# Linear attention on one core: the two signs of a head on the two halves of the partitions

## What is computed

```python
DIM, HEADS, DH, G = (192, 12, 64, 4)
def _phi(x): return concatenate([relu(x), relu(-x)], axis=-1)      # 64 -> 128 features
k = (x @ Wk) ; v = (x @ Wv)                                        # per head 64 columns
q = einsum('bhnd,gde->gbhne', x @ Wq[g], Wt) + bt
q = _ln(gelu(q), gt, betat)
qf, kf = _phi(q) / sqrt(2 * DH), _phi(k)
kv = einsum('bhnd,bhnm->bhdm', kf, v)                              # a table per head: 128 x 64
out = einsum('gbhnd,bhdm->gbhnm', qf, kv)
norm = einsum('gbhnd,bhd->gbhn', qf, kf.sum(axis=2))
out = out / (norm + 1e-6)
fused = gelu(_ln(out @ Wf + bf, gf, betaf)); result = fused @ Wo + bo
```

## Time and profile before

| | |
|---|---|
| median of 3 runs | 2717.93 us (2717.76 to 2718.2) |
| the profiled execution's own time | 2718.29 us |
| its span (first to last instruction) | 2716.4 us |
| busy: PE, DVE | 2542.6 us (94%), 2483.3 us (91%) |
| busy: ACT, POOL | 1392.7 us (51%), 1350.4 us (50%) |
| mean granted TensorE clock | 0.96 |
| L914, table products | 11520 matmuls |
| L1013, features | 640 instructions, mean 672 ns, 384.8 us busy |
| `kv_now` copies | 40 DMAs of 390 KB, 2.6 us to landing |

### The profile page before, as it was taken

One profiled execution on the slowest core, in us unless ns is written; L12 is line 12 of the kernel. 1 busy time (PEld: TensorE's weight loads), 2 busy tenths in 40 slices (PEclk: granted clock), 3 DMA queues, 4 the chain that ended last, 5 costly groups with the idle time before them and its releaser, 6 DMA issues. The chain is left out here.

```text
span 2716.4 us, 74938 instructions
## 1 busy us (share of the span) xinstructions
PE 2542.6 (94%) x29336; PEld 1722.5 (63%) x29336; DVE 2483.3 (91%) x3770; ACT 1392.7 (51%) x2302; POOL 1350.4 (50%) x1019
## 2 busy tenths in 40 slices
PE   4999999788879999999999999999999999999577
PEld 2777777555546666666666666666666666666335
DVE  6999999888889999999999999999999999999583
ACT  5676766555545545545444545545444544554231
POOL 0000000555556666666666666666666766666210
PEclk8999999899989999999999999999999999999765
DMA  7321210211100000000000000000000000000001
GB/s 153 96 51 36 51 35 18 62 36 41 35 7 14 10 8 12 6 12 6 12 6 12 6 12 12 6 12 6 12 6 12 6 12 12 6 12 7 6 0 58
DMA packets 45139, 62.39 MB, mean 23 GB/s; under 512 B 4416, under 2 KB 36160, under 8 KB 44760
## 3 DMA queue, kind: packets, MB, share of 16 engines
q1 hardware_dynamic: 43928, 61.07, 8.5%
q10 hardware_dynamic: 1152, 0.51, 0.1%
HBM read 41.66 MB, written 3.93 MB: 17 GB/s over the span
## 5 line engine op out<-in xcount | busy, mean ns | idle before, releaser
L1231 POOL TENSOR_TENSOR phi_lo<-phi,phi_hi 128x1024 bf16<-128x1024 f32 x240 | 511.2, 2130 | 459.8 <-DVE phi_hi L1112 459.8
L1022 ACT ACTIVATE o_hi<-ps_u 128x512 bf16<-128x512 f32 x240 | 143.3, 597 | 705.1 <-PE ps_u L927 705.1
L941 PE MATMUL ps_y<-staging,o_hi 128*128 128x384 bf16 x1920 | 470.4, 327 | 9.6 <-DVE o_lo L1134 1.9
L941 PE MATMUL ps_y<-staging,o_lo 128*128 128x384 bf16 x1920 | 469.0, 326 | 0.0
L941 PE MATMUL ps_y<-wf_lo,o_hi 128*128 128x384 bf16 x1920 | 468.9, 326 | 0.0
L1224 POOL TENSOR_TENSOR q_ssq<-q_ssq,half 128x8 f32<-128x8 f32 x240 | 405.9, 1691 | 18.8
L1013 ACT ACTIVATE phi<-ps_t,betat,gt 128x512 f32<-128x512 f32 (+1 forms) x640 | 384.8, 672 | 0.8 <-PE ps_t L896 0.8
L1090 DVE SCALAR_TENSOR_TENSOR shared<-q_sum,shared 128x512 f32<-128x512 f32 x240 | 374.3, 1559 | 1.4
L154 PE MATMUL acc<-w_b,feat 128*128 128x384 bf16 x1728 | 295.5, 331 | 42.8 <-DVE w_b L266 39.4
L154 PEld LDWEIGHTS acc<-w_b,feat 128*128 128x128 bf16 x1728 | 168.5, 99 | 158.3 <-DVE w_b L266 40.0
L941 PEld LDWEIGHTS ps_y<-staging,o_lo 128*128 128x128 bf16 x1920 | 187.8, 98 | 124.2
(11 more groups left out here) (218 smaller groups left out, 5664.4 us busy)
## 6 DMA issues: line engine op xcount, KB each, us to landing
kv_now<-kvs SPq DMA_DIRECT2D x40, 390.0 KB, 2.6
xt<-in_x_dram SPq DMA_DIRECT2D x32, 320.0 KB, 5.5
wf_f<-in_wf_dram SPq DMA_DIRECT2D x24, 384.0 KB, 3.2
xt<-in_x_dram SPq DMA_DIRECT2D x32, 256.0 KB, 6.0
out_dram<-h SPq DMA_DIRECT2D x8, 480.0 KB, 2.9
staging<-in_wq_t_dram SPq DMA_DIRECT2D x1, 3072.0 KB, 11.0
staging<-in_tok_w_dram SPq DMA_DIRECT2D x12, 192.0 KB, 8.8
staging<-in_kv_w_dram SPq DMA_DIRECT2D x1, 1536.0 KB, 15.3
```

Source lines behind the costliest of these rows:

```text
L941: last = nc.tensor.matmul(ps_y[:, n, 0:HC], lhs, w[part][:, c, n * HC:(n + 1) * HC], start=c == 0 and lhs is oh and part == 'wf_hi', stop= ...
L1022: nc.scalar.activation(o_hi[:, j % 2], ps_u[:, 0:OC], ACT.Copy).then_inc(s["o_hi_done"], 1)
L1231: nc.gpsimd.tensor_tensor(phi_lo[:, j % 2], phi[:, j % 2], phi_hi[:, j % 2], ALU.subtract).then_inc(s["phi_lo_done"], 1)
```

## The change

The two signs of a head are put on the two halves of the partitions, so that a head's features fill all 128 rows. `features` has to move them there: for each part of an octet (one or two groups), each of the two heads and each of the two signs it has an instruction that reads 64 partitions and writes 64 partitions. The table products then take 128 rows at once. The matmuls read the tables straight from `kv_hi` and `kv_lo` at the batch of the tile; `kv_now` and its DMAs are gone. `accumulate` is changed to match: one matmul makes both signs of a head, with 128 columns of the stationary side.

```diff
@@ accumulate (keys_and_values)
-                    for j in range(HH // 2):
-                        for sign in range(2):
-                            for n, (k, v) in enumerate(((kf_hi, v_hi), (kf_hi, v_lo), (kf_lo, v_hi))):
-                                for side in range(2):
-                                    c = 2 * j + sign
-                                    last = nc.tensor.matmul(
-                                        ps_kv[side * DH:(side + 1) * DH, hf, c * KVW:(c + 1) * KVW],
-                                        k[:, m, 2 * j + side, sign, :], v[:, m, 2 * j + side, :],
...
+                    for j in range(HH):
+                        for n, (k, v) in enumerate(((kf_hi, v_hi), (kf_hi, v_lo), (kf_lo, v_hi))):
+                            last = nc.tensor.matmul(ps_kv[:, hf, j * KVW:(j + 1) * KVW],
+                                                    k[:, m, j].rearrange("p s d -> p (s d)"), v[:, m, j, :],
...
@@ attend
-            @block.sync
-            def _(sp):
-                def tables(tile):
-                    if (n := earlier(tile, NO - 1, NO, NO)) is not None:
-                        sp.wait_ge(s["attended"], n)
-                    sp.dma_start(kv_now[:, :, :, :, :], kvs[:, batch_of(tile.t)]).then_inc(s["kv_in"], 16)
...
@@ attend_octet
-                    if j == 0:
-                        pe.wait_ge(s["kv_in"], 16 * count(tile, 0, 1))
-                    for i in range(PAIRS):
-                        pair = (PAIRS * j + i) % HP
-                        for sign in range(2):
-                            for n, (feature, table) in enumerate(((phi_hi, 0), (phi_hi, 1), (phi_lo, 0))):
-                                for a in range(2):
-                                    rows = slice(a * DH, (a + 1) * DH)
-                                    last = nc.tensor.matmul(
-                                        ps_o[:, a, i * KVW:(i + 1) * KVW],
-                                        feature[rows, j % 2, sign, i * P:(i + 1) * P], kv_now[rows, table, pair, sign, :],
...
+                    b = batch_of(tile.t)
+                    for i in range(OCT):
+                        hd = (OCT * j + i) % HEADS
+                        c = i % PAIRS
+                        out = ps_o[:, i // PAIRS, c * KVW:(c + 1) * KVW]
+                        ph, pl = (v[:, j % 2, i // 2, i % 2, :] for v in (phi_hi, phi_lo))
+                        nc.tensor.matmul(out, ph, kv_hi[:, b, hd, :], start=c == 0, stop=False, skip_group_check=True)
+                        nc.tensor.matmul(out, ph, kv_lo[:, b, hd, :], start=False, stop=False, skip_group_check=True)
+                        last = nc.tensor.matmul(out, pl, kv_hi[:, b, hd, :], start=False, stop=c == PAIRS - 1,
+                                                skip_group_check=True)
@@ features (ACT)
-                    for sign in range(2):
-                        for g, a, b in groups(j):
-                            last = nc.scalar.activation(
-                                phi[:, j % 2, sign, a * P:b * P], ps_t[:, a * P:b * P], ACT.Relu,
-                                bias=w['betat'][:, sign, g:g + 1], scale=w['gt'][:, sign, g:g + 1])
+                    for g, a, b in groups(j):
+                        for head in range(2):
+                            rows = slice(head * DH, (head + 1) * DH)
+                            for sign in range(2):
+                                last = nc.scalar.activation(
+                                    phi[sign * DH:(sign + 1) * DH, j % 2, a:b, head, :],
+                                    ps_t[rows, a * P:b * P].rearrange("p (i n) -> p i n", n=P), ACT.Relu,
+                                    bias=w['betat'][rows, sign, g:g + 1], scale=w['gt'][rows, sign, g:g + 1])
```

More of the change, by code:

```diff
@@ L523, in accumulate @@
                     m = KBUF[2 * t + hf]
-                    for j in range(HH // 2):
-                        for sign in range(2):
-                            for n, (k, v) in enumerate(((kf_hi, v_hi), (kf_hi, v_lo), (kf_lo, v_hi))):
-                                for side in range(2):
-                                    c = 2 * j + sign
-                                    last = nc.tensor.matmul(
-                                        ps_kv[side * DH:(side + 1) * DH, hf, c * KVW:(c + 1) * KVW],
-                                        k[:, m, 2 * j + side, sign, :], v[:, m, 2 * j + side, :],
-                                        start=t == 0 and c == 0 and n == 0,
-                                        stop=t == TPB - 1 and c == HH - 1 and n == 2, skip_group_check=True)
+                    for j in range(HH):
+                        for n, (k, v) in enumerate(((kf_hi, v_hi), (kf_hi, v_lo), (kf_lo, v_hi))):
+                            last = nc.tensor.matmul(ps_kv[:, hf, j * KVW:(j + 1) * KVW],
+                                                    k[:, m, j].rearrange("p s d -> p (s d)"), v[:, m, j, :],
+                                                    start=t == 0 and j == 0 and n == 0,
+                                                    stop=t == TPB - 1 and j == HH - 1 and n == 2, skip_group_check=True)
                     last.then_inc(summed, 1)
@@ L705, in _, with attend @@
                     batch(b, False)
-def attend(nc, w, shared, kvs, stats, h, ident):
+def attend(nc, w, shared, kv_hi, kv_lo, stats, h, ident):
     OCT = 8
@@ L737, in attend @@
         xe = sb("xe3", [P, P], BF16)
-        kv_now = sb("kv_now", [P, 2, HP, 2, KVW], BF16)
         z = sb("z", [P, 2, OCT, DH], F32)
[L740 to L743, removed]
+        phi = sb("phi", [P, 2, PAIRS, 2, P], F32)
+        phi_hi = sb("phi_hi", [P, 2, PAIRS, 2, P], BF16)
+        phi_lo = sb("phi_lo", [P, 2, PAIRS, 2, P], BF16)
+        o = sb("o", [P, 2, PAIRS, DH], F32)
         o_hi = sb("o_hi", [P, 2, OC], BF16)
@@ L854, in attend @@
         with nc.Block() as block:
-            @block.sync
-            def _(sp):
-                def tables(tile):
-                    if (n := earlier(tile, NO - 1, NO, NO)) is not None:
-                        sp.wait_ge(s["attended"], n)
-                    sp.dma_start(kv_now[:, :, :, :, :], kvs[:, batch_of(tile.t)]).then_inc(s["kv_in"], 16)
-                tables(Tile(0))
-                with sp.Fori(1, TILES) as t:
-                    tables(Tile(t))
             @block.tensor
@@ L1787, in early_fusion_kernel @@
             stats = sa("stats", [P, TILES, 2], F32)
-            kvs = sa("kvs", [P, BATCH, 2, HEADS // 2, 2, KVW], BF16)
-            kv_hi, kv_lo = kvs[:, :, 0], kvs[:, :, 1]
+            kv_hi = sa("kvs_hi", [P, BATCH, HEADS, KVW], BF16)
+            kv_lo = sa("kvs_lo", [P, BATCH, HEADS, KVW], BF16)
             w = {'gt': sa("gt", [P, 2, G], F32), 'betat': sa("betat", [P, 2, G], F32), 'gf': sa("gf", [P, INNER // P], F32),
```

17 lines of the change are left out of this document (7 added, 10 removed).

## The result

The changed kernel takes 2847.18 us (median of 4 runs, 2846.49 to 2848.07), the kernel before beside it 2717.85 us: 1.0476 times as long, 95% interval 1.0458 to 1.0494. Slower, as forecast and inside the range of 2728 to 2880, but by 129 us where the sum had 50: the direction was right and the size was off by a factor of 2.6. The time lies in the band that the prediction kept for registers or the weight load (2790 to 2900), and neither of the two brought it there. The profiled execution has a span of 2846.1 us.

The account below looks back on a forecast made before the run. Neither PE nor DVE alone was the bound, but a loop through PE, ACT's gelu and DVE, 43.72 us per tile. From 2718.3 us, features +30, addresses +28 and the rest -8 gave 2768 us; range 2728 to 2880.

Parts of the forecast that it names:

- registers or the weight load: Band of 2790 to 2900 us for address registers or 128-row weight loads dominating PE's table products; chance 0.30.
- the rival of the weight load: PE's table products: 128-row loads do not hide, 55 ns per product, 2820 us; chance 0.30 shared with registers dominating.
- the prediction's estimate by that figure: PE's table products at the skill page's 81 ns per pair: 24 x 81 ns = 1.9 us per octet.
- A single switch: PE, around the table products: switching between half-height and full-height work goes away, 0.2 us per octet.
- Keys and values: Before the attention: one matmul of 128 columns replaces two of 64, equal less two switches, -8 us.
- The 40 DMAs: Per-tile table copies, landing in 2.6 us and needed over 5 us later: hidden, so removing them is worth nothing.
- 8 instructions at the present spacing of 0.457: ACT's features in slots 1 and 4: 3.76 us instead of 1.93, +1.83 in each.
- the loop by slot 4 is shorter: Loop from PE through slot 4's features to DVE: 43.9 us, against 44.48 by slot 1.
- the term of the registers: PE's table addresses in the loop's tiles: 1.5 us per octet, +0.75 us per tile over 37 tiles, +28 us.
- free (2740): PE works table addresses out during the octet before, leaving only the features' cost: 2740 us; chance 0.20 for 2730 to 2750.
- the bound (2875): PE's table addresses at 3.0 us per octet, 48.1 us per tile: 2875 us; chance 0.30 shared with weight load.
- The forecast's loop: PE to slot 1's queries, ACT's features, DVE and back to PE: 44.48 us per tile, +0.76, +30 us over 40 tiles.

Follow-up runs that it names:

- a_fixed: The changed kernel, with the tables copied once per tile to a buffer with fixed addresses; 2808.66 us, 1.0336.
- d: The kernel before, with each feature instruction cut in two at partition 64 and nothing moved; 2788.69 us, 1.0259.
- h_probe: The changed kernel, with feature instructions reordered so that only the half read or the half written changes between neighbours; 2846.47 us in one run.
- e: The changed kernel, with the loop over an octet's query groups innermost in the features; 2809.28 us, 1.034.
- k_alternate: The kernel before, with feature instructions cut in two at partition 64, nothing moved, every neighbour on the other half; 2826.27 us, 1.0402.
- l_grouped: The kernel before, with feature instructions cut in two at partition 64, nothing moved, all of one half before the other; 2774.78 us, 1.0214.
- c_both: The changed kernel, with tables copied to fixed addresses and features written by 128-partition instructions, not moved, so results differ; 2696.42 us, 0.9921.

## Why the prediction came out right in sign and wrong in size

**Right.** The table products of 128 rows start 31 ns apart; the rival of the weight load, at 55 ns per product, is out. The Trainium skill (TensorE: Matmul & The Clock Gate, Back-to-back issue gap) gives about 81 ns for each pair of a weight load and a matmul of 128 columns. The trace's 0.71 us for 23 distances of 65 columns does not agree with the prediction's estimate by that figure. A single switch was worth what was said: in slot 3 it is 0.43 us from the start of the transposes, 1305.36, to the first product, 1305.79, where it was 0.54 before. Keys and values gave 8.6 us for a predicted 8, which is partly luck: over all profiles it is 6 to 9, and the clock has a part in it that is not separated. The 40 DMAs had been hidden: a_fixed, which has 80 of half the size, has no wait for them. DVE idles ahead of L1096 in slots 1 and 4, as said, by 1.80 and 1.39 us (0.5 to 1.4 were forecast). And half the partitions take the same length, 0.55 to 0.56 us.

**Wrong, the step "8 instructions at the present spacing of 0.457".** The spacing was read from neighbours that work on the same 128 partitions, and carried over to neighbours that do not. Measured 4.57 us and not 3.76. This is +0.81 us in slot 1, 32 us over 40 tiles. The experiments d, h, e, k and l show it.

**Wrong, the step "the loop by slot 4 is shorter", at 43.9 us.** It followed the features of slot 4 only to DVE. Behind them in ACT's queue stand the square and the gelu of the fused tile, and PE waits for the latter in slot 5 before it can write its bank. The way over ACT, 0.61 + 4.57 + 0.68 + 1.21 = 7.07 us from the queries of slot 4 to L860 of slot 5, replaces what took 1244.03 - 1237.59 = 6.44 before, or 6.24 with a switch less: +0.83, another 33 us. So both slots lie in one loop, not in two of which the longer counts. That each 0.1 us counts nearly twice is shown by k_alternate and l_grouped. This error costs so much only together with the first: with features of 3.76 us the way over ACT would be 0.61 + 3.76 + 0.68 + 1.21 = 6.26, against 6.24, and would have added 0.02 us per tile.

**Mis-sized, the term of the registers.** 38.5 us (35 by the other pair) for a predicted 28, but made otherwise. I took 16 sums in every octet and placed the stalls in slots 3, 5 and 0, at +0.3, +0.2 and +0.25. There are 16, 16 and 8 in slots 0, 1 and 2 alone. Slot 0 costs 1.73 - 0.71 = 1.02 us per tile and lies in PE's part of the loop; 37 tiles make 38. Slots 1 and 2 lie beside ACT's and DVE's part. The price of one, taken as 0.08, is right where it shows: 1.02 us over 13 gaps. But 3 of the 16 sums in slot 0 and most of those in slot 1 show no gap. That the queue works out addresses only after its wait was not tested; that it cannot keep ahead of products 31 ns apart is shown by slot 0. The places were wrong, and that the sizes are near each other is partly luck. Both rivals on the addresses, free (2740) and the bound (2875), are out; 2847 lies near the second for another reason.

**The sum again.** The forecast's loop, 44.48 us per tile, with the two errors of the features and the addresses in slot 0 is 44.48 + 0.81 + 0.83 + 1.18 = 47.30, where 47.28 was measured (the forecast had 45.2 with its registers); the 1.18 is what PE's 17.11 us from slot 5 to slot 1 have over the sum's 27.75 - 5.58 - 6.24 = 15.93 for that part, of which slot 0 explains 1.02; the other 0.16 were not traced. In terms of the ledger: by the prediction's own loops the features take a tile from 43.72 less one switch, 43.52, to 44.48 us, which is 0.96, or 38 us over 40 tiles; measured are 112. Products of 128 rows in the attention gave 12 us, the 20 less the 8.0 by which c_both's first query (758.27) comes before that of before. Of the two errors the spacing is the one that the other hangs on: it gives 0.81 us per tile by itself, and because the longer features were followed to one consumer and not down their own queue, it counts a second time.

## What to carry to other kernels

On ACT, cut an instruction by partitions only where neighbours keep the same partitions, for source and target alike; the lanes saved gave nothing here, and the order of the pieces alone was worth 38 us here. When a piece of work on an engine grows, go through everything behind it in that engine's queue and ask who waits for that, before saying which loop is the longest. A table that PE reads at a register's address pays at its first uses, here 35 to 38 us; a copy to a fixed address cost no wait where one or two DMAs, issued ahead, carried it, and 71 us of waits where eight did.

## What the hardware showed that I had not expected

- ACT's instructions overlap by about 0.1 us only if the next one reads and writes the same partitions: 0.45 to 0.47 us from start to start for 256 columns, and 0.56 to 0.57 where either half changes. Only the halves 0 to 63 and 64 to 127 were tried. For 4 instructions of 512 columns it is 2.88 us with one change and 3.12 with three.
- A change of source or target partitions alone loses it just as both together do (h_probe, 4.56 us); moving data from one half to the other adds nothing (4.57 with and without).
- PE's stream of a weight load over 128 rows and 65 columns of work keeps 31 ns per product; the 16 address sums of slot 0 put 1.02 us into it, in 13 gaps of 0.08 us each on average.
- 8 DMAs of 48.8 KB land as fast one by one as a single one of 390 KB, but issued in a row they were 1.8 us late where the single one was hidden. Behind that pause of PE 8 tiles took 1.5 us more on top; in one that was looked at, the granted clock fell to 0.63 for 4 us there.
